# Mixture-of-experts routing on one core: the softmax denominator dropped, mask, gate and row weights on ScalarE, work units placed anew

## The reference, cut to what matters

```python
x = x + mamba(layernorm(x))          # in_proj 256->2*512, conv of 4 taps, selective scan with 16 states,
                                     # out_proj, exact gelu, gated linear unit
x = x + ffn(layernorm(x))

# in ffn, x of [T, 256], T = 32 * 512:
shared = (silu(gu[:, :Is]) * gu[:, Is:]) @ shared_down_w
shared = shared * sigmoid(x @ shared_gate_w)
probs = softmax(x @ gate_w)          # [T, 64]
w, idx = top_k(probs, 8)
w = w / sum(w, axis=-1)              # weights of the chosen experts
# pos: the token's place in its expert's queue; only pos < 128 is served
y = sum over the 8 of expert(idx)(x) * w
return y + shared
```

## Time and profile before

| what | value |
|---|---|
| time, median of 3 runs | 4976.88 us (4972.02 to 4981.13) |
| the profiled execution's own time | 4968.66 us |
| its span, first to last instruction | 4966.9 us |
| mean granted TensorE clock | 0.857 of full |
| busy: PE / DVE / ACT / POOL | 3806.3 / 4132.1 / 3220.0 / 4167.7 us |
| DMA | 389.74 MB, mean 78 GB/s |

### The profile page before, as it was taken

How to read it: one execution, slowest core, us unless ns; L and a number is a source line. 1 busy time by engine, 2 the same in 40 slices (tenths; PEclk the granted TensorE clock), 3 DMA queues, 4 the chain that set the end, 5 groups by cost and what they waited for, 6 DMA issues and landing times.

```text
span 4966.9 us, 56503 instructions
## 1 busy us (share of the span) xinstructions
PE 3806.3 (77%) x16000; PEld 2357.7 (47%) x16000; DVE 4132.1 (83%) x4214; ACT 3220.0 (65%) x4799; POOL 4167.7 (84%) x2223
## 2 busy tenths in 40 slices
PE   4677888877877878887877878887877878876465
PEld 2444445544444445454544445554444445543343
DVE  3888998888889999888888998888888998885433
ACT  4666777766667777676767777776667777763111
POOL 4988899888888899888888899888888898883476
PEclk7788888888888888888888888898888888888767
DMA  2122112222222112222222112222222102220566
GB/s 108 73 84 74 57 48 77 84 84 80 84 84 77 55 41 83 84 84 80 84 84 82 55 37 81 84 84 80 84 84 83 59 35 78 79 79 11 144 156 135
DMA packets 138165, 389.74 MB, mean 78 GB/s; under 512 B 14496, under 2 KB 97632, under 8 KB 104560
## 3 DMA queue, kind: packets, MB, share of 16 engines
q1 hardware_dynamic: 123504, 362.73, 20.0%
q0 software_dynamic: 14336, 23.08, 2.5%
HBM read 333.17 MB, written 52.59 MB: 78 GB/s over the span
## 4 chain that ended last, share of the span: by engine, by line
POOL 55%; issue 27%; DVE 8%; PE 5%; ACT 2%; DMA 1%; POOLq 1%; SPq 0%; DVEq 0%; ACTq 0%
POOL hs L375 31%; POOL hs L384 14%; DVE ps L1164 3%; POOL dt L425 3%; POOL dtu L429 3%; DVE hs L1164 1%; POOL rstd L397 1%; DVE stats L1036 1%; POOL hs L469 1%; PE ps L799 1%; PE ps L909 1%; DVE small L1102 1%; POOL out L492 1%; PE ps L843 1%; POOL hs L484 1%
## 5 line engine op out<-in xcount | busy, mean ns | idle before, releaser
L375 POOL TENSOR_TENSOR hs<-dtu,b_all 128x1024 f32<-128x1024 f32 x1024 | 2397.0, 2361 | 67.0 <-PE ps L799 63.1
L533 ACT ACTIVATE ps<-dt,neg_a 128x512 f32<-128x512 f32 x2048 | 1328.4, 683 | 670.3 <-DVE hs L1174 338.6
L799 PEld LDWEIGHTS ps<-ident,hs 128*128 128x128 f32 x8192 | 1058.4, 155 | 606.2 <-issue 431.3
L1164 DVE TENSOR_TENSOR_SCAN ps<-ps,hs 128x1024 f32<-128x1024 f32 x544 | 1242.8, 2285 | 88.2 <-POOL hs L375 67.6
L384 POOL TENSOR_TENSOR hs<-hs,c_all 128x1024 f32<-128x1024 f32 x480 | 1132.6, 2360 | 212.9 <-DVE hs L1164 212.9
L799 PE MATMUL ps<-ident,hs 128*128 128x128 f32 x8192 | 1190.2, 296 | 134.6 <-POOL hs L384 133.8
L1164 DVE TENSOR_TENSOR_SCAN hs<-ps,hs 128x1024 f32<-128x1024 f32 x480 | 1087.5, 2277 | 51.4 <-ACT ps L533 44.7
L909 PE MATMUL ps<-mT,w_sgu 128*128 128x512 f32 x1024 | 616.3, 734 | 311.0 <-DVE hid L1121 201.7
L1174 DVE TENSOR_TENSOR hs<-ps,c_all 128x1024 f32<-128x1024 f32 x544 | 666.0, 1224 | 35.5
L909 PEld LDWEIGHTS ps<-mT,w_sgu 128*128 128x128 f32 x1024 | 212.9, 231 | 505.9 <-DVE hid L1121 212.8
L823 PE MATMUL ps<-xnT,w_in 128*128 128x512 f32 x512 | 295.2, 706 | 124.1 <-DVE xc L1054 121.6
(11 more groups left out here) (132 smaller groups left out, 4750.7 us busy)
## 6 DMA issues: line engine op xcount, KB each, us to landing
b_all<-bc SPq DMA_DIRECT2D x128, 1024.0 KB, 8.0
c_all<-bc SPq DMA_DIRECT2D x128, 1024.0 KB, 9.7
table<-rows SPq DMA_DIRECT2D x32, 640.0 KB, 12.8
xin<-x SPq DMA_DIRECT2D x32, 512.0 KB, 3.5
out<-mT SPq DMA_DIRECT2D x32, 512.0 KB, 3.7
c_all<-egu_w SPq DMA_DIRECT2D x64, 256.0 KB, 2.9
c_all<-edown_w SPq DMA_DIRECT2D x64, 128.0 KB, 3.0
counts<-cnt SPq DMA_DIRECT2D x32, 128.0 KB, 2.4
```

The source lines that it names most:

```text
L375: pool.tensor_tensor(ring(h, hf, n), dtu[:, JH * hf:JH * hf + JH, :], b_all[:, n, :].unsqueeze(1).broadcast_to([P, JH, L]), ALU.mult)\
L533: i = act.activation(state_of(n)[:, k, :], dt[:, j, :], ACT.Exp, scale=neg_a[:, j, n:n + 1])
L799: m = pe.matmul(ybank[:, i, k * P:(k + 1) * P], ring(h, hf, n)[:, k, i * P:(i + 1) * P], ident[:, :], start=False, stop=(n == N - 1), is_t ...
L1164: dve.tensor_tensor_scan(inputs if s in ON_POOL else whole, whole, inputs, 0.0, ALU.mult, ALU.add).then_inc(state_ready, 1)
```

## The change

The routing computes no softmax denominator. ACT's exponentials drop their sums; DVE takes the eight largest of the exponentials themselves, and the weights are exponential over the sum of the eight. ACT adds 1 for the shared gate. Two operations go to ACT in a new unit `weights` at step 26: the mask as Relu of the negated `rep` (1 where an entry was replaced by -1, else 0), and the weights, which are now written for all 64 experts of a token; only chosen ones are ever read. `choose` on DVE keeps a reciprocal of the gate, the eight largest, their replacement, the sum of eight and its reciprocal, and moves to step 25. SP's store of `rows` and PE's count wait for new semaphores. The rest of the diff changes the tables of steps: which read-outs are POOL's (15 as before), and where the units stand.

```diff
         maskb = sb("maskb", [P, NT, E], BF16)
-        small = sb("small", [P, 6, NT])
+        small = sb("small", [P, 4, NT])
...
         outb = mT[:, :, :].rearrange("p f l -> p (f l)")
-        negmax, esum, rsum, s8, eg, gate_s = (small[:, i, :] for i in range(6))
+        negmax, s8, eg, gate_s = (small[:, i, :] for i in range(4))
...
         exp_ready = sem("exp_ready")
+        mask_ready, weights_ready = sem("mask_ready"), sem("weights_ready")
...
             def store_rows(q):
-                sp.wait_ge(route, ROUTES * q + ROUTES)
+                sp.wait_ge(weights_ready, q + 1)
...
             def router_exp(q):
-                act.wait_ge(route, q * ROUTES + 2)
-                for i in range(NT):
-                    act.activation(pr[:, i, :], lg[:, i, 0:E], ACT.Exp, bias=negmax[:, i:i + 1],
-                                   accum_out=esum[:, i:i + 1])
+                act.wait_ge(route, q * ROUTES + 1)
+                for i in range(NT):
+                    act.activation(pr[:, i, :], lg[:, i, 0:E], ACT.Exp, bias=negmax[:, i:i + 1])
                 act.activation(eg.unsqueeze(2), lg[:, :, E:E + 1], ACT.Exp, scale=-1.0).then_inc(exp_ready, 1)
+                act.wait_ge(exp_ready, 2 * q + 1)
+                act.activation(gate_s, eg, ACT.Identity, bias=1.0).then_inc(exp_ready, 1)
+
+            def weights(q):
+                act.wait_ge(route, q * ROUTES + 3)
+                act.activation(maskb[:, :, :], rep[:, :, :], ACT.Relu, scale=-1.0).then_inc(mask_ready, 1)
+                act.wait_ge(route, q * ROUTES + ROUTES)
+                for i in range(NT):
+                    m = act.activation(rows[:, i, DM:ROW], pr[:, i, :], ACT.Identity, scale=s8[:, i:i + 1])
+                m.then_inc(weights_ready, 1)
...
                     router_exp(q)
+                if s == WEIGHTS:
+                    weights(q)
...
             def count(q):
-                pe.wait_ge(route, q * ROUTES + MASK_STEP)
+                pe.wait_ge(mask_ready, q + 1)
...
                 dve.wait_ge(post_read, q * POST_USES + POST_R + 1)
-                dve.tensor_reduce(negmax, lg[:, :, 0:E], AX.X, ALU.max, negate=True).then_inc(route, 2)
+                dve.tensor_reduce(negmax, lg[:, :, 0:E], AX.X, ALU.max, negate=True).then_inc(route, 1)
...
             def choose(q):
-                at = [q * ROUTES + 2]
-
-                def link(i):
-                    i.then_inc(route, 1)
-                    at[0] = at[0] + 1
-                    wait_apart(dve, route, at[0])
-
-                def wide(t, w):
-                    return t.unsqueeze(2).broadcast_to([P, NT, w])
-
-                dve.wait_ge(exp_ready, q + 1)
-                dve.reciprocal(rsum, esum)
-                link(dve.tensor_scalar(gate_s, eg, 1.0, None, ALU.add))
+                dve.wait_ge(exp_ready, 2 * q + 2)
                 dve.reciprocal(gate_s, gate_s)
-                link(dve.tensor_tensor(pr[:, :, :], pr[:, :, :], wide(rsum, E), ALU.mult))
...
                     k = dve.max(top[:, i, :], pr[:, i, :])
-                link(k)
-                for i in range(NT):
-                    dve.match_replace(rep[:, i, :], top[:, i, :], pr[:, i, :], -1.0)
-                link(dve.tensor_reduce(s8, top[:, :, :], AX.X, ALU.add))
-                dve.reciprocal(s8, s8)
-                link(dve.tensor_tensor(rep[:, :, :], rep[:, :, :], pr[:, :, :], ALU.not_equal))
-                link(dve.tensor_copy(maskb[:, :, :], rep[:, :, :]))
-                link(dve.tensor_tensor(pr[:, :, :], pr[:, :, :], rep[:, :, :], ALU.mult))
-                dve.tensor_tensor(rows[:, :, DM:ROW], pr[:, :, :], wide(s8, E), ALU.mult).then_inc(route, 1)
+                k.then_inc(route, 1)
+                wait_apart(dve, route, q * ROUTES + 2)
+                for i in range(NT):
+                    k = dve.match_replace(rep[:, i, :], top[:, i, :], pr[:, i, :], -1.0)
+                k.then_inc(route, 1)
+                dve.tensor_reduce(s8, top[:, :, :], AX.X, ALU.add).then_inc(route, 1)
+                dve.wait_ge(route, q * ROUTES + 4)
+                dve.reciprocal(s8, s8).then_inc(route, 1)
...
 
-ON_POOL = (0, 1, 6, 10, 13, 14, 15, 16, 18, 20, 22, 23, 24, 26, 30)
-
-ROUTES, MASK_STEP = 10, 8
+ON_POOL = (0, 6, 10, 11, 13, 14, 15, 18, 19, 22, 23, 24, 27, 28, 31)
+
+ROUTES = 5
...
 AFTER_X = 1
-AFTER_Z = 2
-AFTER_S = 2
-AFTER_D = 1
+AFTER_Z = 1
+AFTER_S = 0
+AFTER_D = 0
...
 AFTER_MT = 2
-AFTER_XT = 1
-AFTER_R = 2
+AFTER_XT = 0
+AFTER_R = 1
 AFTER_SG = 1
-AFTER_SU = 2
+AFTER_SU = 1
...
 NORM0 = 1
-SUM_X = 14
-MOMENTS0 = 18
-SCALES0 = 29
-SIZES = (29, 10)
-INPUTS = (29, 10)
+SUM_X = 18
+MOMENTS0 = 23
+SCALES0 = 25
+SIZES = (29, 9)
+INPUTS = (29, 9)
...
 X_AT = (4, 5, 18, 19)
-Z_AT = (7, 9, 12, 14)
-SKIP_AT = (31, 12)
+Z_AT = (6, 12, 13, 15)
+SKIP_AT = (30, 17)
 SILU_X = 21
-SILU_Z = 17
+SILU_Z = 28
...
 S_AT = 23
-D_AT = 24, 24, 0, 1
-SOFT_AT = ((26, 28), (6, 7))
+D_AT = (24, 25, 0, 0)
+SOFT_AT = ((25, 27), (4, 7))
...
 M_AT = (5, 6)
-G_AT = (8, 9)
+G_AT = (7, 9)
 V_AT = (10, 11)
-MT_AT = (12, 12)
-XT_AT = (15, 16)
+MT_AT = (12, 13)
+XT_AT = (16, 16)
...
 ROUTER_EXP = 20
-SG_AT = (19, 20, 21, 22)
-SU_AT = (23, 24, 25, 26)
-CHOOSE = 23
+SG_AT = (17, 19, 20, 22)
+SU_AT = (24, 25, 26, 27)
+WEIGHTS = 26
+CHOOSE = 25
```

## The result

The kernel after takes 4656.89 us (median of 4 runs, 4646.89 to 4665.34), the kernel before 4974.45 us (median of 4). The ratio is 0.9362, 95% interval 0.9337 to 0.9387: 6.4% faster. The prediction said 4590 us with a range of 4515 to 4720 us. Direction and stated range hold; the gain is 317.6 us where the sum had 388.6 us, and the time lies 17 us above the 4550 to 4640 us that the forecast itself was given.

A forecast was written before the change was run, and what follows sets the result against it. POOL was taken as the bound, with 495.0 us of waits to win; less 22.4 us that stay and 84 us of new waits, the gain is 388.6 us: 4590 us, own range 4550 to 4640, stated range 4515 to 4720.

The forecast's parts named there:

- What bounds the kernel: Loop over sequences: POOL's work per sequence is fixed, so only its idle time, waits of 495.0 us together, can be won.
- The 7 us: POOL's 7.04 us wait before a read-out: DVE's 128x4 add stands until POOL runs dry, then POOL idles through `choose`.
- Item 2: ACT gains the add of 1, four scalings and the mask: between 1 and 2.3 us a turn, in its idle time.
- item 3: The skill advises against moving such work to ACT (71 us, nothing won); L1102's 8 us of standing on DVE weighs more.
- Item 4: `SU_AT` and `AFTER_SU`: PE's sum that frees input 31's slot is issued ahead of the projection; the 1.87 us wait goes.
- Item 5: Step sizes: an earlier logarithm removes POOL's 4.51 us wait; `SIZES[1]` at 9 adds a wait of 1.4 us.
- Item 6: `ON_POOL` and `MT_AT`: the moments' 2.0 us go; DVE and POOL nearly even, charged 1.4 us, bounds 0 and 5.5 us.
- The sum: Whole kernel: gain 388.6 us, period 127.6 us a turn, time 4588 us, rounded to 4590; chance 0.45.
- 4674 us for a lock of one operation: Rival on DVE's stand: the lock lasts one POOL operation at most, only the short turn's gain is sure; chance 0.04.
- DVE becomes the bound: Rival on the loop: DVE's load, L909 and small waits make 131.6 us a turn, 4717 us in all; chance 0.20.
- the slower case: Rival: ACT's waits gather before the logarithm of step 27; at 17 us the time is 5025 us; chance 0.03.
- 4504 us: Rival on POOL's waits: no new wait at all, since DVE has 10 us to spare; chance 0.15.

The follow-up runs named there:

- after_flat: The kernel after with all turns written out, no loop over sequences; 4557.08 us (ratio 0.9169).
- after_loop4: The kernel after with four turns in one iteration of the loop over sequences instead of two; 4597.1 us (ratio 0.9248).

## Why the prediction was right, and where its size was off

- **What bounds the kernel.** Right: POOL's work is unchanged and the whole gain is POOL's waits, 312.3 us of them against 310.0 us of time.
- **The 7 us.** Right as to the mechanism: no kept instruction stands, and the waits for scans went from 212.9 to 28.2 us with the routing alone. The expectations "below 40 us in all" (105.0 us) and "a period of 126 to 129 us" (130.2 us) failed for the kernel after, because of the jump; without it they are 36.1 us and 126.3 us.
- **Item 2, ACT.** A mask takes 0.40 us, a scaling 0.33, the add 0.21; ACT's busy time rose by 26.3 us, 0.8 us a turn, where 1 to 2.3 were taken. So item 3 weighed rightly: the add alone, put back on DVE, costs 23 us.
- **Item 4, the ring slot.** The wait went, 63.1 to 1.7 us. Either half alone removes most of it (19.6 and 13.6 us are left).
- **Item 5, the logarithm.** The 4.5 us went, but one of the two reasons given was wrong. A short `choose` does not bring the logarithm forward: with the routing alone the wait grew to 176.7 us, since POOL came earlier as well. The new places did it (91.4 us with them alone); which of them was not separated. The new wait of 1.4 us in the other half is there: 1.2 us in after_flat's turns.
- **Item 6, even places.** The moments' wait went, by the places alone. The near-tie was charged 1.4 us; in after_flat it is 1.1 us.
- **The sum.** Its 127.6 us a turn came to 126.3 us where nothing else interferes, and 4588 us to 4557 us. The kernel after has 130.2 us. The missing term is 3.9 us a turn, 99.8 us between after and after_flat: the loop's jump. Item 6 asked what the moved read-outs do to POOL and DVE, not what they do to PE, whose wait of 3.16 us for read-out 30 covered the jump. In the kernel before there was no such stand on PE, so no row had a price for it, and an overhead hidden behind a wait was put at nothing. The two errors pull against each other: 99.8 us left out and 4588 - 4557 = 31 us charged too much by the other terms; the rest, 69 us, is what 4588 us lies below the result.
- **The range.** The result is outside the forecast's own 4550 to 4640 us. That the stated range held it is in part luck: it reached up to 4720 us for the sake of rivals that did not happen. The rival nearest in number, 4674 us for a lock of one operation, is not the reason: no kept instruction stands at all.
- **The rivals.** "DVE becomes the bound" would have looked alike in POOL's waits, several us at read-outs for DVE. after_flat tells it apart: with the same DVE work, most of the waits are gone (105.0 us have become 36.1). The 5025 us of the slower case have no working; 17 us in each of 30 turns on top of 4504 us would make 5014.

## What to carry to other kernels

Where VectorE works beside a busy GpSimd, look for short instructions with long medians and wide spreads, and look at them as a class: the stand of the one that was moved away passed to the next. What one of them costs depends on its place. When a wait goes, list what ran under its cover on every engine, the loop's own jump among it, and price it as if it were bare; a table entry that moves work from one engine to another takes away the waits of a third. A rhythm in the turn lengths with the period of the loop's body is worth one experiment with a different unrolling before any story about clocks.

## What the runs showed of the hardware that was not expected

- A jump back of a loop with a body of two turns left PE without work for 2.5 to 3.2 us at all 13 jumps of the kernel after, and ACT for 2.4 to 2.7 us at 8 of them. On PE it cost more than itself: with the low clock behind it and the next turn's, 99.8 us between the two kernels over 13 jumps, 7.7 us each. (The written-out turns also hold constants where the loop computes addresses. That is worth little: in after_loop4, which still computes them, all turns away from a jump but one last 126.3 to 126.9 us, against 126.3 us.) What the engines do during the stand, no view shows.
- A 128x4 SBUF-to-SBUF add on DVE stood 8.3 us in the median beside a busy GpSimd in one place and 1.6 us in another, and multiplies with two SBUF operands 8.1 and 2.3 us; as four adds of 128x1 it took 0.14 us each and never stood. What makes the long stand pass several ends of GpSimd operations is open.
- Holding up PE's mean granted clock (0.872 to 0.915) with idle work did not shorten the kernel.
